# Attention with two experts per token: the last query group's probabilities turned in 32x32 squares by VectorE and placed by DMAs

## What is computed

```python
x = L0_attn_x                                  # (8, 1024, 256) float32
xn = layernorm(x)
qkv = einsum('bse,ehd->bshd', xn, w_qkv)       # 16 heads, q, k, v of 64
logits = q @ k.T / sqrt(64), causal mask       # per batch and head, 1024 x 1024
probs = softmax(logits)
attn = einsum('bshd,hde->bse', probs @ v, w_out)
moe = top-2 of 8 experts, capacity 2048, 256 -> 1024 -> 256, relu
out = x + attn + moe
```

## Time and profile before

| | us |
|---|---|
| median of 3 runs | 3411.4 |
| the profiled execution | 3409.17 |
| its span | 3407.2 |
| PE busy over the span | 3273.8 (96%) |
| DVE, ACT, POOL busy | 2065.9, 1966.9, 1466.7 |
| mean granted TensorE clock | 0.981 |

### The profile page before, as it was taken

The page is one execution under the profiler, slowest core; times in us unless marked ns, Lnnn a source line. Parts: engine busy times, 40 slices in busy tenths (PEclk is TensorE's granted clock), DMA queues, the critical chain, the costliest instruction groups (busy, mean ns, idle before and its releaser), DMA issues.

```text
span 3407.2 us, 66117 instructions
## 1 busy us (share of the span) xinstructions
PE 3273.8 (96%) x23061; PEld 2739.5 (80%) x23061; DVE 2065.9 (61%) x5471; ACT 1966.9 (58%) x4244; POOL 1466.7 (43%) x1999
## 2 busy tenths in 40 slices
PE   5499999999879999999999999999999999999999
PEld 3489998999858888888888888888888888888887
DVE  6844434444246666666666666666666666666666
ACT  2344444444346666666666666666666666666665
POOL 2131221212035554555555555555555555555554
PEclk7799999999989999999999999999999999999999
DMA  6122222221143333333333323433343233324321
GB/s 198 33 79 69 74 75 67 72 70 49 45 103 84 80 81 85 84 84 96 71 82 85 96 69 83 97 87 69 81 106 77 69 93 95 80 68 101 81 66 44
DMA packets 197064, 274.76 MB, mean 81 GB/s; under 512 B 53328, under 2 KB 153744, under 8 KB 196752
## 3 DMA queue, kind: packets, MB, share of 16 engines
q1 hardware_dynamic: 184464, 237.08, 28.2%
q0 software_dynamic: 12288, 33.57, 3.4%
HBM read 102.80 MB, written 33.55 MB: 40 GB/s over the span
## 4 chain that ended last, share of the span: by engine, by line
PE 71%; DMA 1%; ACT 0%; DVE 0%; SPq 0%; issue 0%; POOL 0%; ACTq 0%
PE S L1183 18%; PE O L1213 16%; PE T L1195 15%; PE W L1107 8%; PE W L1140 4%; PE W L1122 3%; PE S L1122 3%; PE S L1107 3%; PE S L1140 1%; PE S L1130 0%; DMA ql<-kk 0%; ACT pr L1255 0%; DMA kk<-qq 0%; DMA xnt<-xn 0%; DVE kk L1327 0%; DVE S L1343 0%
## 5 line engine op out<-in xcount | busy, mean ns | idle before, releaser
L1412 POOL TENSOR_SCALAR pr<-pr,rinv 128x128 f32<-128x128 f32 (+7 forms) x1024 | 766.7, 750 | 1136.1 <-DVE rinv L1302 1136.1
L1343 DVE CUSTOM_DVE_ANT_0 S<-S,late 128x128 f32<-128x128 f32 (+7 forms) x1024 | 780.3, 763 | 298.2 <-PE S L1183 289.2
L1255 ACT ACTIVATE pr<-S,negm 128x128 f32<-128x128 f32 (+7 forms) x1024 | 759.3, 741 | 274.8 <-DVE negm L1343 251.2
L1195 PE MATMUL T<-ident,pr 128*128 128x128 f32 x4608 | 671.6, 273 | 0.6 <-ACT pT L1243 0.5
L1243 ACT ACTIVATE pT<-T 128x512 f32<-128x512 f32 (+3 forms) x768 | 416.8, 543 | 320.6 <-PE T L1195 315.6
L1183 PE MATMUL S<-kk,qq 128*128 128x256 f32 (+2 forms) x1536 | 591.8, 385 | 3.4 <-ACT pr L1255 2.5
L1195 PEld LDWEIGHTS T<-ident,pr 128*128 128x128 f32 x4608 | 540.6, 140 | 53.4 <-issue 14.4
L1213 PE MATMUL O<-pT,vv 128*64 128x256 f32 (+1 forms) x5120 | 582.6, 365 | 0.1
L1183 PE MATMUL S<-kk,ql 128*128 128x256 f32 (+2 forms) x1536 | 515.1, 343 | 0.0
L1213 PEld LDWEIGHTS O<-pT,vv 128*64 128x64 f32 x5120 | 333.9, 136 | 201.0 <-issue 54.6
L1243 DVE COPY pT<-T 128x128 f32<-128x128 f32 (+3 forms) x768 | 366.0, 477 | 42.9 <-PE T L1195 42.5
(11 more groups left out here) (182 smaller groups left out, 6072.8 us busy)
## 6 DMA issues: line engine op xcount, KB each, us to landing
ql<-kk SPq DMA_DIRECT2D x256, 256.0 KB, 3.6
kk<-qq SPq DMA_DIRECT2D x128, 256.0 KB, 2.8
qq<-qq SPq DMA_DIRECT2D x128, 256.0 KB, 3.0
y<-yb SPq DMA_DIRECT2D x128, 128.0 KB, 1.7
wr<-in_L_attn_w_qkv SPq DMA_DIRECT2D x128, 128.0 KB, 2.9
x<-in_L_attn_x SPq DMA_DIRECT2D x16, 512.0 KB, 5.4
xn<-xn SPq DMA_DIRECT2D x16, 512.0 KB, 5.5
w1r<-in_L_ffn_w SPq DMA_DIRECT2D x8, 1024.0 KB, 5.1
```

The lines of the kernel that those rows point to most:

```text
L1195: ins = e.transpose(T[ch % 2][:, b * P:(b + 1) * P], pr[slot(n, s)][:, kt * P:(kt + 1) * P], k["ident"][:])
L1255: e.activation(pr[i][:, 0:w], S[s % 2][:, off:off + w], ACT.Exp, bias=negm[:, i:i + 1], scale=-1.0, accum_out=rsum[:, i:i + 1]).then_inc(e ...
L1343: e.tensor_tensor_reduce(masked, masked, late[:, SEQ - w:], 1.0, -MASKED, ALU.add, ALU.min, negm[:, i:i + 1]).then_inc(negmax.sem, 1)
L1412: e.tensor_scalar(pr[i][:, 0:width(s)], pr[i][:, 0:width(s)], rinv[:, i:i + 1], 1.0, ALU.mult, ALU.mult).then_inc(scaled.sem, 1)
```

## The change

Only `attention_and_sum` changes. Steps 12 to 15 of a unit (query group 3; `WIDE` is 12) are no longer turned by PE. Instead:
- DVE (`square`) turns the scaled row buffer of the step in squares of 32x32 into a new tile `squares`, 2 steps behind (`SQUARE_LAG`). Each square is turned, but still stands in its old 32 partitions.
- SP (`place`) moves the squares to their rows: 16 DMAs, one for each pair of source and target quarter, 32 partitions x 4 x 256 elements (128 KB) each. They start when all four steps are squared and groups 0 and 1 of the unit are done, since the target is the buffer `pT_odd`, seen as `wide`.
- `values` for group 3 waits for these DMAs (`placed`) and reads its moving operand in runs of 32 elements.

Beside that, the probabilities are turned 4 steps behind and the ring has 5 row buffers; a group's product is one run (`PART` 8); `v0` and `v1` make the half pair for unit n+1, so that `v2` and `v3` are not made ahead of unit 0; the mask `late` is BF16; the tables are new.

```diff
-    STEPS, LAG, RING = 2 * QT, 3, 6
+    STEPS, LAG, RING = 2 * QT, 4, 5
-    PART = 4
+    PART = 8
+    WIDE = STEPS - STEPS // GROUPS
+    BL = 32
+    QUARTERS = P // BL
-    STEP_OF = {'xn': 0, 'p0': 1, 'o2': 2, 'p1': 2, 'p2': 4, 'p3': 6, 'v0': 6, 'v1': 8, 'o3': 10, 'o0': 11, 'o1': 13}
+    STEP_OF = {'v0': 1, 'p0': 3, 'p1': 3, 'p2': 4, 'xn': 4, 'v1': 5, 'o2': 6, 'p3': 6, 'o3': 9, 'o0': 13, 'o1': 15}
-    AFTER = [10, 11, 15, 19]
+    AFTER = [9, 14, 17, 23]
-    BEFORE = ["p0", "p1", "p2", "p3", "v0", "v1", "v2", "v3"]
+    BEFORE = ["p0", "p1", "p2", "p3", "v0", "v1"]
...
-        pT = two(lambda h: two(lambda g: sb(f"pT{h}{g}", [P, QT - 2 + 2 * g, GQ])))
+        pT_even, pT_odd = (sb(f"pT{g}", [P, 2, QT - 2 + 2 * g, GQ]) for g in range(2))
+        pT = [[t[:, h] for t in (pT_even, pT_odd)] for h in range(2)]
+        wide = pT_odd[:].rearrange("p h k q -> p (h k q)").rearrange("p (x a r) -> p x a r", x=4, a=QUARTERS)
+        sq = sb("squares", [P, 4, QUARTERS, QT, BL])
-        late = sb("late", [P, SEQ])
+        late = sb("late", [P, SEQ], BF16)
+        wide_of = lambda h, kt, t: wide[:, 2 * h + t:2 * h + 2, :, kt * BL:(kt + 1) * BL].rearrange("p t a i -> p (t a) i")
...
+            def place(n):
+                e.wait_ge(squared.sem, squared.at(n, STEPS - WIDE))
+                e.wait_ge(pv.sem, pv.at(n, GROUPS - 2))
+                for a in range(QUARTERS):
+                    for b in range(QUARTERS):
+                        e.dma_start(wide[b * BL:(b + 1) * BL, :, a, :],
+                                    sq[a * BL:(a + 1) * BL, :, b].rearrange("p x k i -> p x (k i)")).then_inc(placed.sem, 16)
...
+                if n > 0:
+                    place(n - 1)
                 if n + 1 < UNITS:
                     spread(n, 0)
...
-                W, pair = work_bank(name), n // 2 + 1
-                i = int(name[1]) + 2 * (n % 2 if n >= 0 else 0)
+                W, pair = work_bank(name), (n + 1) // 2
+                i = int(name[1]) + 2 * ((n + 1) % 2)
...
+                    if g == GROUPS - 1:
+                        e.wait_ge(placed.sem, placed.at(n, 16 * QUARTERS * QUARTERS))
...
+                        turned_p = wide_of(h, kt, a // P) if g == GROUPS - 1 else pT[h][g % 2][:, kt, a:GQ]
...
-                if 0 <= lagged(n, s)[0] < UNITS:
+                if 0 <= lagged(n, s)[0] < UNITS and lagged(n, s)[1] < WIDE:
                     turn_p(*lagged(n, s))
...
+            def square(n, s):
+                x, KT = s - WIDE, s // 2 + 1
+                if x == 0 and n > 0:
+                    e.wait_ge(placed.sem, placed.at(n - 1, 16 * QUARTERS * QUARTERS))
+                e.wait_ge(scaled.sem, scaled.at(n, s + 1))
+                e.transpose(sq[:, x % 2 * 2 + x // 2, :, 0:KT, :],
+                            pr[slot(n, s)][:, 0:KT * P].rearrange("p (k b i) -> p b k i", b=QUARTERS, i=BL)).then_inc(squared.sem, 1)
```

More of the change, by code:

```diff
@@ L849, in pieces @@
             return BEFORE
[L850 removed]
+        there = {"p": n + 1 < UNITS, "x": n + AHEAD < TILES, "v": n + 1 < UNITS}
         return [p for p in STEP_OF if there.get(p[0], n < UNITS if p in ("o0", "o1") else n > 0)]
@@ L984, in attention_and_sum @@
         kept = two(lambda i: Count(sem(f"s_kept{i}"), CHUNKS // 2))
+        squared = Count(sem("s_squared"), STEPS - WIDE)
+        placed = Count(sem("s_placed"), 16 * QUARTERS * QUARTERS)
         pv = Count(sem("s_pv"), GROUPS)
@@ L1019, in attention_and_sum @@
         ALL = [(n, s) for n in range(UNITS) for s in range(STEPS)]
-        END = [(UNITS, s) for s in range(12)]
+        END = [(UNITS, s) for s in range(16)]
         @block.sync
@@ L1263, in work @@
                 elif name[0] == "v":
-                    i, pair = int(name[1]) + 2 * (n % 2 if n >= 0 else 0), n // 2 + 1
+                    i, pair = int(name[1]) + 2 * ((n + 1) % 2), (n + 1) // 2
                     if pair >= 2:
@@ L1348, in _ @@
                     reciprocal(UNITS - 1, STEPS - 1)
-                if 0 <= lagged(n, s)[0] < UNITS:
+                if 0 <= lagged(n, s)[0] < UNITS and lagged(n, s)[1] < WIDE:
                     keep(e, *lagged(n, s), 1)
+                if 0 <= squaring(n, s)[0] < UNITS and squaring(n, s)[1] >= WIDE:
+                    square(*squaring(n, s))
                 for name in pieces(n):
@@ L1372, in split_wv @@
                 e.wait_ge(wvload.sem, wvload.at(m, 32))
-                e.wait_ge(filled.sem, filled.at(*((2 * m - 1, "v1") if m else (-1, "v3"))))
+                e.wait_ge(filled.sem, filled.at(2 * m, "v1"))
                 for c_ in range(MC):
@@ L1415, in _ @@
                     split_w(n + 1)
-                if s == STEP_OF["v1"] + 1 and n % 2 == 1 and n // 2 + 2 < UNITS // 2:
-                    split_wv(n // 2 + 1)
+                if s == STEP_OF["v1"] + 1 and n % 2 == 0 and n // 2 + 1 < UNITS // 2:
+                    split_wv(n // 2)
                 if s == 0:
```

36 lines of the change are left out of this document (21 added, 15 removed).

## The result

The changed kernel takes **3489.8 us** (median of 4 runs, 3487.42 to 3502.56) against 3411.1 us before in the same session: a ratio of the means of 1.0239, 95% interval 1.0213 to 1.0264. It is slower by 79 us, where 3347 was forecast, 64 us faster, with a range of 3225 to 3450. The profiled execution has a span of 3485.6 us.

What follows compares the result with a forecast made beforehand. PE alone was taken to set the time, busy 1899.81 of 1900 us. 63 units x -1.3 = -82, start -5, end +10, batch starts +13 gave -64 us, 3347 us by the median; range 3225 to 3450.

Steps and rivals of the forecast that it cites:

- PE's work, 34.3 us: PE's work per unit falls from 37.99 us by 3.19 for removed turned blocks and 0.5, to 34.3.
- the 0.5 us for joined runs: On PE, fewer runs and fewer changes of matmul form save 0.4 to 0.6 us a unit, taken as 0.5.
- Two exp waits, 0.9 and 1.2 us: PE's scores of step 12 wait 0.9 us for exp of step 10, those of step 1 wait 1.2 for step 15.
- Squares at 1.15 us, the last one done at 7.4: On DVE, each square takes 1.15 us start to start; step 15's ends 7.4 us after step 15 starts on PE.
- Issue rate 0.6 us: SP issues the placing DMAs 0.6 us apart, so sixteen take 9.6 us plus a landing.
- The placing, 12.0 us: Sixteen DMAs of 128 KB, awaited by group 3, take 12.0 us, with ends of 11.3 and 14.5.
- the first rival: The placing becomes the bound: slower once it takes over 13.0 us; at 14.5 about 3505 us. Chance 0.18.
- its sign of being wrong: The forecast is wrong if PE's wait for the placing is over 1.5 us a unit.
- The second rival: Waits are smaller than reckoned, down to PE's 34.3 us a unit, about 3195 us; middle of the case 3270. Chance 0.20.
- Moving operand in runs of 32: It slows group 3 on PE by up to 3.4 us, 3550 us; chance 0.07 together with squares twice as dear.
- Batch starts, 13 us: At seven batch starts a 256 KB refill just ahead of the placing costs 1.9 us each, 13 us.
- Ends: Kernel start saves 5 us (3 to 9) of PE's wait for the first load; the end costs 10 us more.

Runs made afterwards that it cites:

- e1: Changed kernel with only the four placing DMAs of equal source and target quarter issued, the other twelve left out; 3305.4 us.
- e5: Changed kernel with its new order kept, but PE turns all sixteen steps and nothing is squared or placed; 3497.2 us.
- e9: Changed kernel with sixteen placing DMAs that each carry only half of the row, 64 KB instead of 128 KB; 3365.1 us.
- e3: Changed kernel with POOL's two gathers of 128 KB a unit issued in steps 9 and 11 instead of 1 and 3; 3398.9 us.

## Why the prediction was wrong

- **PE's work, 34.3 us**: right in sum (34.3 in e1), with a split that is not: the 0.5 us for joined runs is not seen in e5, and the removed blocks take 3.9 us off PE's work instead of 3.19. That the two errors cancel is luck.
- **Two exp waits, 0.9 and 1.2 us**: right in place, 0.62 and 1.16 us in size (the unit without any placing wait is 36.14 in e1, 36.4 by the forecast). The round of scores, maximum and exp was read properly from the earlier trace rows.
- **Squares at 1.15 us, the last one done at 7.4**: right (1.10 for 896 columns, 1.23 for 1024; mean 1163 ns over 256; done at 7.3). The Trainium skill, "VectorE: DVE Perf Modes", section on the three transpose paths, gives 311 ns for one 128x128 in bf16, which would be 2.5 us for eight blocks; here a float32 row of eight takes 1.23 us. The prediction called the 272 ns of a copy "mostly fixed cost"; by its own 1.06 ns a column the fixed part is 136 ns, half.
- **Issue rate 0.6 us**: 0.65 (10.42 us for sixteen). It looks right for one and is 0.8 us over sixteen.
- **The placing, 12.0 us: the step that failed.** I had by bytes "10.2 at 205 GB/s, plus 1.0 until bytes move and 0.6 for the last landing", and by issue "16 x 0.6 = 9.6 plus a landing, the same", and took agreement of two estimates for a confirmation. They are two limits that hold at once. The issues with half of the bytes (e9) give 12.5, with 0.8 more for the issue rate than reckoned; the other 1.2 us is bytes and what shares the engines. The gathers in it are 0.6 at the median and 0.9 on the mean (e3), where 0.2 to 0.5 was put for them and the wakings. The median is 13.65 and the mean 13.84, above the break-even of 13.0 that the first rival named. The term by bytes was too dear, not too cheap: the packets fill the engines for 8.9 us, not 10.2. Group 3 stood at 21.0 after step 15 instead of 19.4, and PE, which arrived as forecast (19.2 against 19.1), waited 2.07 us instead of 0.3. This is over the 1.5 us that the prediction named as its sign of being wrong.
- **The clock: a term that was missing.** Group 3 at 1.2 GHz behind PE's wait, some 1.7 us longer in 26 of 64 units, 0.69 us a unit. A wait on PE was priced at its length; here it cost more than its length. By unit: 36.4 and 0.3 of wait were forecast, 36.14, 2.07 and 0.69 of clock were found.
- **The first rival was the right one**, though its 3505 us are near the result partly by luck: it took 14.5 for the placing. By its own price of 64 us for each us over 13.0 the mean of 13.84 gives 3465; the clock, which it did not have, adds 43, and the cheaper rest of the unit (36.14 against 36.4) takes off 16: 3492. It had a chance of 0.18. What spoke for it (kilobyte runs, gathers, a margin of 1 us) had been written down; what spoke against it (issue rate and 205 GB/s) were the two limits added up too kindly. A margin of 1 us between a sum of eight terms and PE's arrival, with 64 us for each us missed, deserved a chance near one half.
- **The second rival** (smaller waits, about 3270): no. Even without any placing wait the kernel would be at 3305.
- **Moving operand in runs of 32**: costs nothing, 3.46 us for 32 products in either layout where the clock is full.
- **Batch starts, 13 us**: right in size, another way. At the seven batch starts group 2's distance is 40.6 us, 1.9 more than in the other units, but in e1 it is the same everywhere. So the refill costs only through the placing: PE waits 2.80 us there instead of 1.89, and six of the seven met the low clock.
- **Ends**: step 15 of the first unit comes at 1000.04 us instead of 1005.71, 5.7 earlier (forecast 5), and from step 15 of the last unit to the end it is 3485.6 - 3455.71 = 29.9 us, 12.3 more than before (forecast 10), most of it the last placing, bare: group 3 waits 10.88 us there.
